# A fused feed-forward, causal attention and feed-forward layer on one core: side work placed in later query blocks

## What is computed

```python
x = x + 0.5 * ffn(layernorm(x))
x = x + attention(layernorm(x))       # 16 heads of 16, causal, q and k layer-normed per head, softmax, Wo, bo
x = x + 0.5 * ffn(layernorm(x))       # same weights as the first
# ffn: base_W x + base_b, plus a shared rank-16 pair, plus six rank-16 experts,
# of which the two with the highest softmax gate are kept and weighted
```

## Time and profile before

| | |
|---|---|
| median of three runs | 1363.42 us |
| the profiled execution, its own time | 1358.05 us |
| its span, first to last instruction | 1356.3 us |
| TensorE (PE) busy | 1164.8 us, 86% |
| ScalarE (ACT) busy | 1021.1 us, 75% |
| VectorE (DVE) busy | 458.1 us, 34% |
| GpSimd (POOL) busy | 232.9 us, 17% |
| mean granted TensorE clock | 0.958 |

### The profile page before, as it was taken

The page is one execution under the profiler, slowest core; times in us unless marked ns, Lnnn a source line. Parts: engine busy times, 40 slices in busy tenths (PEclk is TensorE's granted clock), DMA queues, the critical chain, the costliest instruction groups (busy, mean ns, idle before and its releaser), DMA issues.

```text
span 1356.3 us, 23146 instructions
## 1 busy us (share of the span) xinstructions
PE 1164.8 (86%) x9076; PEld 382.2 (28%) x9076; DVE 458.1 (34%) x1164; ACT 1021.1 (75%) x1132; POOL 232.9 (17%) x377
## 2 busy tenths in 40 slices
PE   2636877889889998999989998999999999999984
PEld 2522432323323232232322222222222222121222
DVE  4655537356444533443234232122222011010114
ACT  2203555567677878788888997899999999999960
POOL 2223432222222122211022002102102001000000
PEclk9768898999999999999999999999999999999996
DMA  4011200300210021000200001100001100000000
GB/s 129 1 55 32 72 1 26 85 0 2 74 37 2 1 77 35 1 1 17 74 23 1 1 1 56 40 1 1 1 1 47 49 2 1 0 1 1 9 9 16
DMA packets 39673, 33.39 MB, mean 25 GB/s; under 512 B 8786, under 2 KB 39496, under 8 KB 39560
## 3 DMA queue, kind: packets, MB, share of 16 engines
q1 hardware_dynamic: 37360, 31.74, 8.0%
q10 hardware_dynamic: 2200, 0.12, 0.1%
HBM read 18.73 MB, written 12.85 MB: 23 GB/s over the span
## 4 chain that ended last, share of the span: by engine, by line
PE 61%; ACT 14%; DVE 11%; issue 8%; POOL 1%; DMA 1%; SPq 1%; ACTq 1%; DVEq 0%; POOLq 0%
PE ps L1088 56%; ACT ring L695 14%; PE ps L1127 2%; PE ps L1188 1%; DVE oT L1068 1%; DVE xnT L767 1%; DMA x<-in_x 1%; PE ps L1296 1%; DVE st L726 1%; SPq L527 1%; PE ps L1304 1%; PE ps L1147 1%; DVE xnT L765 1%; DVE area L747 1%; DVE att L1075 1%
## 5 line engine op out<-in xcount | busy, mean ns | idle before, releaser
L695 ACT ACTIVATE ring<-ps 128x1024 f32<-128x1024 f32 x1056 | 989.7, 1107 | 178.5 <-PE ps L1088 175.8
L1088 PE MATMUL ps<-ring,vf 128*17 128x512 f32 (+3 forms) x4608 | 566.0, 569 | 2.9 <-POOL ring L649 2.0
L1088 PE MATMUL ps<-queries,keys 50*128 50x512 f16 (+3 forms) x2304 | 380.4, 371 | 34.3 <-DMA queries<-shift_d 9.9
L1088 PEld LDWEIGHTS ps<-queries,keys 50*128 50x128 f16 x2304 | 93.5, 93 | 504.1 <-ACT ring L695 425.5
L649 POOL TENSOR_SCALAR_AFFINE_SELECT ring<-ring 128x256 f32<-128x256 f32 (+1 forms) x224 | 95.6, 443 | 434.0 <-ACT ring L695 432.9
L1088 PEld LDWEIGHTS ps<-ring,vf 128*17 128x17 f32 x4608 | 80.1, 96 | 173.5 <-issue 148.1
L765 DVE CAST xnT<-ps 128x512 f16<-128x512 f32 x50 | 34.5, 691 | 160.8 <-PE ps L1127 115.4
L1068 DVE COPY oT<-ps 128x512 f32<-128x512 f32 x32 | 22.1, 690 | 165.9 <-PE ps L1088 165.6
L899 DVE SCALAR_TENSOR_TENSOR x<-ps,power,x 128x512 f32<-128x512 f32 x32 | 24.0, 750 | 124.2 <-PE ps L1088 124.2
L461 POOL TENSOR_TENSOR sq<-area 128x512 f32<-128x512 f32 x32 | 33.7, 1052 | 184.4 <-DVE ss L904 89.7
L1088 PE MATMUL ps<-baseT,xnT 128*128 128x256 f16 x384 | 56.6, 287 | 8.1 <-DVE qT L932 2.7
(11 more groups left out here) (145 smaller groups left out, 703.7 us busy)
## 6 DMA issues: line engine op xcount, KB each, us to landing
parts_d<-split SPq DMA_DIRECT2D x32, 256.0 KB, 2.6
keys<-parts_d SPq DMA_DIRECT2D x96, 64.0 KB, 2.3
queries<-parts_d SPq DMA_DIRECT2D x192, 32.0 KB
x<-in_x SPq DMA_DIRECT2D x8, 512.0 KB, 3.9
out_x<-x SPq DMA_DIRECT2D x16, 256.0 KB, 2.2
queries<-shift_d SPq DMA_DIRECT2D x64, 4.0 KB
ring<-in_base_W SPq DMA_DIRECT2D x1, 256.0 KB, 4.6
ring<-in_Wq SPq DMA_DIRECT2D x1, 256.0 KB, 5.8
```

The costliest lines, as they stand in the source:

```text
L695: act.activation(probs[:, u % RING, :], bank(2 * (u % SLOTS), 2), ACTF.Exp, bias=0.0, scale=1.0).then_inc(exp_ok, 1)
L1088: return pe.matmul(o, lhsT, rhs, start=start, stop=stop, skip_group_check=True)
```

## The change

`tail(c)` is split into `output(c)` (the four turnout and projout steps) and `back(c)` (the second feed-forward and the load). Where each part goes:

- `output(c - 1)` stays in block c, but on its units 4 to 7 instead of spread out.
- `back(c)` goes from block c + 1 to block c + 2, from its tenth unit on. Block 7 takes `back(5)` and then `back(6)`; `back(7)` stays behind the attention.
- `front(0, 0, n)` for n = 4 to 7 goes from block n - 2 to block n - 1, where it stands ahead of `prepare(n)` in one chained list. For n = 2 and 3 it stays in block n - 2.

No instruction is added or removed: the same steps stand in another order.

```diff
+LONG = 3
...
-def tail(c):
+def output(c):
+
     for stage in ("turnout", "projout"):
         for a in range(2):
             yield 1.5, stage, (c, a)
+
+
+def back(c):
+
     yield from front(1, 2, c)
     yield 0, "load", c + XS
...
         lists = []
+        u0, u1 = UNIT0[c], UNIT0[c + 1]
         if c + 1 < NC:
-            lists.append(spread(prepare(c + 1), UNIT0[c], max(UNIT0[c + 1] - 12, UNIT0[c] + 6)))
-        if c + 2 < NC:
-            lists.append(spread(front(0, 0, c + 2), UNIT0[c], UNIT0[c + 1] - 2))
+
+            ahead = front(0, 0, c + 1) if c >= LONG else ()
+            lists.append(spread(itertools.chain(ahead, prepare(c + 1)), u0, max(u1 - 12, u0 + 6)))
+        if c + 2 <= LONG:
+            lists.append(spread(front(0, 0, c + 2), u0, u1 - 2))
         if c >= 1:
-            lists.append(spread(tail(c - 1), UNIT0[c] + 4, UNIT0[c + 1] - 1))
+            lists.append(spread(output(c - 1), u0 + 4, u0 + 8))
+        behind = [c - 2] if 2 <= c < NC - 1 else [c - 2, c - 1] if c == NC - 1 else []
+        if behind:
+            lists.append(spread(itertools.chain(*map(back, behind)), u0 + 10, u1 - 2))
...
-    for _, stage, n in tail(NC - 1):
+    for _, stage, n in itertools.chain(output(NC - 1), back(NC - 1)):
         yield stage, n
```

More of the change, by code:

```diff
@@ L3 @@
 from contextlib import ExitStack
+import itertools
 import math
```

## The result

The changed kernel takes 1348.42 us, the median of four runs (1347.32 to 1348.64), against 1361.75 us for the kernel before in the same series (1358.17 to 1364.60). The ratio is 0.9915 with a 95% interval of 0.9891 to 0.9939: 0.85% faster, clear of the 0.5% that I had called no change. My likeliest case, no change, did not come; the side that came is that of rival 1, for a part of its reasons. Carried over to the median from which I forecast, the ratio gives 0.9915 x 1363.42 = 1351.8 us, just inside the low end of the range.

A forecast was written before the change was run, and what follows sets the result against it. TensorE was taken to bind early and in blocks 3 to 5, ScalarE late, notably in block 7. Terms summed to -0.5 us, giving 1357.6 us profiled; medians lie 5.4 higher, so 1363 us, with 1350 to 1375 for 8 in 10.

The forecast's parts named there:

- no change: Whole kernel: about 1363 us, within 0.5% (6.8 us) of before; chance 0.43.
- rival 1: Faster: a third list was the trouble in blocks 1 and 2; 1353 to 1356 us, chance 0.32.
- the signs that I had named: Profile checks: block 7 under 235 us or block 6 under 214 means wrong prices; block 1 clock under 0.9 means Rival 4.
- Block 2: Losing front(4) saves 9.1 us of matmuls and 2.6 of idle time, -11.7; the output steps add 0.6.
- Block 6: Gaining front(7) costs 10.7 us, 2 of it waiting for x, bounds 8.7 and 14.5; output steps add 0.9.
- Block 7: A second feed-forward there costs 5.6 us, bounds 5.6 and 8.7; the output steps add 3.1.
- the burst: Output steps on four units: 2.3 us of waits each; net +0.1, +0.6, 0.9 in blocks 3 to 6, +3.1 in 7.
- Block 1: Losing back(0) saves 9.2 us of matmuls and 3.3 of idle time, -12.5; the output steps add 0.1.
- the waits for x in blocks 3 to 5 stay: Blocks 3 to 5: load issued just before the block's end in both orders, so no cost; only 0.9 each for output.
- rival 3: Feed-forward ahead of prepare waits so long for x that the block's start stands still; no chance of its own.
- Rival 2: Slower: each burst of output steps costs 5 us in place of 2.3; +12, 1376 us, chance 0.20.
- Rival 4: Slower: clock in blocks 1 and 2 falls towards 0.79; +34 us in full, +11 for a third, 1374 us; chance 0.03.

The follow-up runs named there:

- front_only: Against the kernel before, only the first feed-forward moves a block later, chained ahead of prepare; output and second feed-forward stay spread over block c + 1: 1339.61 us.
- the pair with the later start: front_only_later compared with chain_later, to price the first feed-forward in blocks 2 and 6; they took 1333.82 and 1341.52 us.
- chain_later: chain_only with its chained list starting 8 units later from block 2 on: 1341.52 us.
- burst_only: The kernel before with only the output steps put on units 4 to 7 and the second feed-forward behind them in the same block: 1376.30 us.
- output_spread: The changed kernel with the four output steps spread (u0 + 24 for u0 + 8) instead of on units 4 to 7: 1345.56 us.
- late_back5: The kernel before with only back(5) moved from block 6 to block 7, spread and with no load in play: 1360.30 us.
- chain_only: The kernel before with front(c + 2) chained ahead of prepare(c + 1) in the same block, from block 2 on: 1368.37 us.
- start_later: The changed kernel with the chained list of first feed-forward and prepare starting 8 units later in blocks 3 to 6: 1331.69 us.
- front_only_later: front_only with its chained list starting 8 units later in blocks 3 to 6: 1333.82 us.
- back_sooner: The changed kernel with the second feed-forward and load spread over the first 62% of blocks 2 to 5: 1338.28 us.
- later_spread: start_later with the four output steps also spread instead of on units 4 to 7: 1321.36 us.

## Why the prediction was right or wrong, point by point

**Which engine binds where** was read rightly, and so was the direction of every block but 5: 1 and 2 down, 3, 4, 6 and 7 up. The sizes were not, and in the sum they partly cancel: the forecast was too low by 4.9 us in block 1, too high by 9.0 in block 2, by 2.9 in block 6 and by 3.5 in block 7, and too low by 1.3 over blocks 3 to 5. That the time stayed inside the range is in part this luck. Of the signs that I had named, block 7 came out under 235 us, so its price was wrong; block 6 did not fall under 214, though the price of `front(7)` was wrong as well.

**Block 2 (forecast -11.1, measured -20.1)** is the term that turned the sign. I priced the front's idle time by its share of the bank's uses, 6/32, 2.6 us. TensorE's idle time fell from 13.8 us to 98.7 - 93.14 = 5.6, more than half. Two waits of TensorE that before had in block 2 are gone in the changed kernel and in `front_only`:

```profile
PE ps L1304 <- DVE att L1075: 3.0, 1, 3.0
PE ps L1188 <- DVE area L767: 2.7, 1, 2.7
```

The second belongs to a `heads` step. The first is the one to learn from. In the trace of before VectorE waits 2.1 us for the x of `front(4)`, until 266.54 us, then does those moments, and only then divides; the turnout waits for that. I said that this wait goes from block 2, and charged 2 us for the one that comes in block 6, but gave block 2 no credit: a slip in the sum, which with it would have come to -2.5 us. Over its first 24 units block 2 fell from 37.1 to 29.3 us, 7.8 of its 20.1. TensorE's busy time fell by 11.9, not 9.1; the granted clock of the block went from 0.96 to 1.00, so the rest of the work probably became quicker too. My upper bound, 14.5 us, was too low for the move alone from the order of before (18.5, `front_only`) and only just reached by the pair with the later start (14.7). Idle time in a queue of steps is not shared out by their number.

**Block 6 (forecast +11.6, measured +8.7)**: my lower bound for the front, 8.7 us of matmuls, was no bound. It cost 6.5 to 8.3 us. In the pair that gives 6.5, TensorE is busy 204.0 us in block 6 with it and 198.0 without, and its idle time grows by 0.5; so the matmuls themselves add only 6.0 us to TensorE's time, and the 8.7 of the earlier trace rows was too high. That ScalarE hides a part of them there is not shown. The 14.5 us from blocks 5 to 6 was the wrong row: it compares two blocks of different lengths, and what block 5 paid for its crowded start and its three lists (7.3 us, `chain_later`) was in it.

**Block 7 (forecast +8.7, measured +5.2)**: the burst was sized well, +3.1 forecast and 234.5 - 231.7 = 2.8 measured (3.9 in `burst_only`). The second feed-forward cost 2.4 (`output_spread` against before) to 3.5 (`late_back5`), not 5.6. Here something is hidden: in `late_back5` TensorE's busy time grows by 5.5 us in block 7 and its idle time falls by 2.0. My stretches also held two divides, which come in any case; how much of the 5.6 us was theirs no run shows. A small slip beside it: the 15.5 us that I took for seven groups of the earlier trace rows are the sum of all eight.

**Block 1 (forecast -12.4, measured -7.5)**: taking `back(0)` out gave 98.5 - 87.0 = 11.5, near the 12.5. The burst, which I had at +0.1, cost 4.0. It is not 2.3 us everywhere: in block 2 it costs nothing (98.7 us against 100.2 with the output spread), and no run shows why.

**Blocks 3 to 5 (forecast +2.7, measured +0.8, +7.1 and -3.9)**: here the step that failed is "the waits for x in blocks 3 to 5 stay", a term that I put at nothing; what came is my rival 3, to which I gave no chance. I took the load's place in the list for its time. SyncE walks the same list with its own backlog: in the trace of before, which I could have asked, it issued the loads 1.5 to 2.0 us after the block's start, and in the changed kernel that of x of block 4 came 2.4 us and that of block 5 6.1 us after blocks 3 and 4 had begun. And I left out what stood ahead of the waiting moments: before, those of `prepare` did and covered part of the wait, which is 3.7 against 2.1 us where the load is equally late (block 2 of `chain_only`). For block 4, where the wait grew by 5.9 us, the later issue is 4.6 of it. This cost about 11 us over four blocks, if `start_later` and `front_only_later` may be subtracted, with the clock's fall in it. In block 5 the dearer start, 5.4 us over the first 24 units, was more than made up behind it: `front_only` is 5.2 us shorter than before there and `chain_only` 5.2, so the chained list is the likely cause of the block's fall.

**The rivals.** Rival 1's result came nearest (1353 to 1356 us against 1351.8 by the ratio); of its two reasons, block 2 was even dearer than it said, while block 1 gained 11.5 and not 14.4, and "third list" is the wrong name: `chain_only` has two lists and the same block 2. Rival 2's burst is real, `burst_only` lost 14.7 us, but in the changed kernel spreading it gave only 2.9 back. Rival 4 did not come: block 1 was granted 0.92, less than before's 0.95 but over the 0.9 that I had named. The clock did fall elsewhere, to 0.86 over the first 24 units of block 4, where TensorE had stood for 7.1 us in one piece. That is the direction that the Trainium skill, "TensorE: Matmul & The Clock Gate", section "What's actually happening", gives: idle time brings the throttled state back. Of the thinner early blocks, block 1 went the way that I had weighed it for, from 0.95 to 0.92, and block 2 the opposite, from 0.96 to 1.00, with its idle time down from 13.8 to 5.6 us.

What stays open: why two lists in place of three help in block 5 and not in block 2, why the burst is dear in block 1, and how much of the calmer start's 6 us is VectorE's queue and how much the bank.

## What to carry to other kernels

When work is moved between stages, price it by the idle time and clock that a stage shows with and without it, not by its busy time: the same feed-forward cost 14.7 us in block 2 and 6.5 in block 6. A step's place in a common list is not its time on every engine; look at the DMA-issuing queue's backlog where the load is placed, and at which instruction waits first for it and what stands behind that one. A change whose parts gain and lose should be run in parts: here one part alone was worth 22 us, the whole 13, and the whole, with the late start and the spread output mending most of its two losses, 40.

## What the hardware showed that I had not expected

The 45 to 48 us behind the attention hold the same 116 matmuls in these versions, and the lower the granted clock of that stretch, the longer it is. The last row of the table of stretches for back_sooner, start_later and later_spread, in this order:

```profile
1291.80:1336.50 44.70, 19.68 (x116) 13.19 (x116) 17.98 (x45) 0.22 (x1) 2.10 (x3) 0.69 0.04 12
```

```profile
1282.00:1330.00 48.00, 22.97 (x116) 14.62 (x116) 17.98 (x45) 0.22 (x1) 2.09 (x3) 0.57 0.03 11
```

```profile
1272.50:1320.00 47.50, 22.35 (x116) 14.37 (x116) 18.00 (x45) 0.25 (x2) 2.10 (x3) 0.60 0.03 12
```

At 0.69 the end takes 44.7 us, at 0.57 48.0, and TensorE's busy time grows by the same 3.3 us, from 19.68 to 22.97. No edit made this difference between versions, and it is the size of several effects that I looked for. The block table tells such edits apart better than the total, within the 2 to 3 us by which a block itself varies.
